# Two 64-row tiles for the logits and adjacency products of a two-step graph kernel

## The reference, cut to what matters

```
q = X @ W1.T @ W2.T;  k = X @ W3.T;  logits = q @ k.T          # width 64
probs = softmax(logits); keep the largest until their sum passes 0.9; A = renormalised
R = (adj + I) / rowsum(adj + I)
for n in (0, 1):
    A  = top_p_attention(Xa)
    Xf = R @ Xf;   Xa = A @ Xa
    Z += Xf @ U1[n].T + Xa @ U2[n].T
out = layernorm(x + layernorm(x + Z) * g + b)
```

## Time and profile before

| | |
|---|---|
| median of 3 runs | 1667.79 us (1663.79 to 1667.81) |
| profiled execution, its own time | 1664.64 us |
| its span, first to last instruction | 1662.8 us |
| TensorE busy | 1531.0 us, 92% |
| VectorE busy | 1266.9 us, 76% |
| ScalarE busy | 779.7 us, 47% |
| GpSimd busy | 244.0 us, 15% |
| mean granted TensorE clock | 0.956 of full |
| rank stage one, rank stage two | about 20 to 320 us, 786 to 1152 us |

### The profile page before, as it was taken

How to read it: one execution, slowest core, us unless ns; L and a number is a source line. 1 busy time by engine, 2 the same in 40 slices (tenths; PEclk the granted TensorE clock), 3 DMA queues, 4 the chain that set the end, 5 groups by cost and what they waited for, 6 DMA issues and landing times. The chain is left out here.

```text
span 1662.8 us, 17981 instructions
## 1 busy us (share of the span) xinstructions
PE 1531.0 (92%) x4753; PEld 887.4 (53%) x4753; DVE 1266.9 (76%) x3735; ACT 779.7 (47%) x1237; POOL 244.0 (15%) x283
## 2 busy tenths in 40 slices
PE   7999999979999999998999999998259879899996
PEld 4556556434555555554566666565135445455553
DVE  6788888723677777776799999999868787787664
ACT  4555555412556565564444444444134434445444
POOL 2010210241000000001001111112310221312222
PEclk9999999989999999998999999999569999999998
DMA  7556566644444555555556766672000000000000
GB/s 266 176 154 155 154 171 188 192 180 140 166 173 187 208 208 188 185 202 205 187 155 200 190 182 186 178 177 79 3 2 1 1 8 7 1 7 7 7 7 13
DMA packets 53452, 211.94 MB, mean 127 GB/s; under 512 B 22464, under 2 KB 31232, under 8 KB 32880
## 3 DMA queue, kind: packets, MB, share of 16 engines
q1 hardware_dynamic: 49872, 210.61, 40.7%
q0 software_dynamic: 3488, 0.31, 0.2%
HBM read 206.64 MB, written 4.50 MB: 127 GB/s over the span
## 5 line engine op out<-in xcount | busy, mean ns | idle before, releaser
L1289 ACT ACTIVATE psL<-psL,umax 128x1024 f32<-128x1024 f32 x256 | 278.5, 1088 | 297.1 <-DVE umax L1812 297.0
L1818 DVE MAX8 cand<-psL 128x8 f32<-128x256 f32 (+1 forms) x640 | 372.4, 584 | 57.4 <-PE psL L916 52.1
L915 PE MATMUL psL<-kA,mq 128*128 128x512 f32 x512 | 299.5, 585 | 2.5 <-ACT psL L1289 1.6
L885 PE MATMUL psO<-adj_in,xn 128*128 128x512 f32 x512 | 242.7, 597 | 3.8 <-DMA adj_in<-in_adjT 2.1
L885 PE MATMUL psO<-adj_in,xf 128*128 128x512 f32 x512 | 241.9, 597 | 4.4 <-POOL adj_in L611 4.4
L1097 PE MATMUL psO<-ebuf,xn 128*128 128x512 f32 x512 | 241.5, 593 | 0.5 <-DVE ebuf L2029 0.5
L2029 DVE SCALAR_TENSOR_TENSOR ebuf<-ebuf 128x1024 f32<-128x1024 f32 x128 | 156.7, 1225 | 109.0 <-PE psO L1097 92.2
L1449 ACT ACTIVATE ebuf<-psL 128x1024 f32<-128x1024 f32 x128 | 130.5, 1022 | 187.8 <-PE psL L1143 153.4
L916 PE MATMUL psL<-kB,mq 66*128 66x512 f32 x512 | 203.8, 398 | 0.0
L1398 ACT ACTIVATE ebuf<-psL 128x1024 f32<-128x1024 f32 x128 | 130.9, 1023 | 129.3 <-PE psL L1064 128.9
L1155 PE MATMUL psO<-xf,xa 128*128 128x512 f32 x340 | 167.6, 617 | 5.7 <-DVE xf L2182 5.6
(11 more groups left out here) (341 smaller groups left out, 1962.3 us busy)
## 6 DMA issues: line engine op xcount, KB each, us to landing
adj_in<-in_adjT SPq DMA_DIRECT2D x128, 1024.0 KB, 5.0
adj_in<-in_adj SPq DMA_DIRECT2D x32, 2048.0 KB, 7.6
xaT<-in_xT SPq DMA_DIRECT2D x4, 512.0 KB, 5.4
xa_dram<-xa SPq DMA_DIRECT2D x8, 256.0 KB, 7.8
out<-t SPq DMA_DIRECT2D x8, 256.0 KB, 2.3
list_dram<-ids,place POOLq DMA_INDIRECT x64, 9.3
rel_prob<-cut_dram SPq DMA_DIRECT2D x32, 2.0 KB
cut_dram<-ncut SPq DMA_DIRECT2D x16, 2.0 KB, 8.8
```

The costliest lines, as they stand in the source:

```text
L885: last = nc.tensor.matmul(psO[:], fs[:, j, :], adj_in[:, r % RING, j % JQ, :], start=(j == 0), stop=(j == JT - 1))
L915: nc.tensor.matmul(o, qA[:, t * P:(t + 1) * P], kA[:, c:c + BI], start=True, stop=False)
L1289: nc.scalar.activation(ps[:], ps[:], ACT.Exp, bias=umax[:, bass.ds(i * UB + k, 1)], scale=1.0, accum_out=usum[:, bass.ds(i * UB + k, 1)]). ...
L1818: last = v.max(cand[:, t % 2, at + c * 8:at + c * 8 + 8], psL[(turn + k) % 3][:, c * WIDE:(c + 1) * WIDE])
```

## The change

In both rank stages, logits and adjacency products are issued as matmuls of 64 rows on either half of the array, each half into a PSUM bank of its own.

- Logits: a unit is now six matmuls, three on partitions 0 to 63 into an even bank (the unit's first 512 columns) and three on partitions 64 to 127 into an odd bank (the second 512). `kB` grows to 128 partitions and holds, besides hi(k), the lo and hi parts in the half where each tile needs them; the lower half is put back with one copy (`k_restore`) at the stage's end, the rows of ones with a memset on GpSimd.
- Key units: a second ScalarE copy and a second VectorE difference for each; GpSimd's copy is half as wide.
- Adjacency: a call becomes two 64-row calls, into `psO` and `psO_odd`. ScalarE makes two copies at a group's end, and GpSimd adds them (`join_flow`, signal `r_o_sum`) before transposes or z terms read the flow. The two groups of step one outside the rank stage stay as they were.
- Banks: `psO_odd` takes a bank of the third unit buffer. Units take turns in two buffers, and TensorE waits for the exponential of unit k-2.
- Order: step one's transposes come three units later; the first block's adjacency counts in step two change to (0, 0, 2 x 5, 3 x 4, 2 x 5).

```diff
+        banks = pb("banks", [P, 6, BI])
+        psL = [banks[:, 2 * b:2 * b + 2, :].rearrange("p h c -> p (h c)") for b in range(3)]
         psO = pb("psO", [P, BI])
+        psO_odd = banks[:, 5, :]
+        def unit_banks(w):
+            first = 2 * ((w + 1) % 2)
+            return first, first + 1
...
+                def join_flow(i):
+                    pool.wait_ge(g["r_o_sb"], i + 1)
+                    pool.sem_inc(met, 1)
+                    flow = flowT[:, i * BI:(i + 1) * BI] if s == 0 else oT[:]
+                    nc.gpsimd.tensor_tensor(flow, flow, flow_odd, ALU.add).then_inc(g["r_o_sum"], 1)
...
+                JOIN_BEFORE = {0: 0, 1: 1, 3: 2, 4: 3, 5: 4, 7: 5}
...
-                    last = nc.tensor.matmul(psO[:], fs[:, j, :], adj_in[:, r % RING, j % JQ, :],
-                                            start=(j == 0), stop=(j == JT - 1))
+                    if s > 0 or i < FLOWS:
+                        low_rows = nc.tensor.matmul(psO[:], fs[0:DA, j, :], adj_in[0:DA, r % RING, j % JQ, :],
+                                                    start=(j == 0), stop=(j == JT - 1))
+                        high_rows = nc.tensor.matmul(psO_odd, fs[DA:P, j, :], adj_in[DA:P, r % RING, j % JQ, :],
+                                                     start=(j == 0), stop=(j == JT - 1))
...
+                def two_tiles(even, odd, hi, lo, u, landed):
+                    c = u * UNIT
+                    first, second = slice(c, c + BI), slice(c + BI, c + UNIT)
+                    low, high = slice(0, DA), slice(DA, P)
+                    nc.tensor.matmul(even, hi[low], kA[low, first], start=True, stop=False)
+                    nc.tensor.matmul(odd, hi[high], kA[high, second], start=True, stop=False)
+                    nc.tensor.matmul(even, hi[low], kB[low, second], start=False, stop=False)
+                    nc.tensor.matmul(odd, hi[high], kB[high, second], start=False, stop=False)
+                    nc.tensor.matmul(even, lo[low], kB[low, first], start=False, stop=True).then_inc(landed, 1)
+                    nc.tensor.matmul(odd, lo[high], kB[high, second], start=False, stop=True).then_inc(landed, 1)
...
-                            if not (prev is None and k < 3):
-                                pe.wait_ge(g["r_exp_done"], i * UB + k - 2)
+                            if i * UB + k >= 2:
+                                pe.wait_ge(g["r_exp_done"], i * UB + k - 1)
...
+                            even, odd = unit_banks(i * UB + k)
+                            two_tiles(banks[:, even, :], banks[:, odd, :], qA[:, t * P:(t + 1) * P], qB[:, t * P:(t + 1) * P],
+                                      u, g["r_l_ps"])
...
                 def k_hi(of, u):
                     act.wait_ge(of["k_ps"], u + 1)
-                    nc.scalar.copy(kA[:, u * UNIT:(u + 1) * UNIT], psL[k_bank(u)][:]).then_inc(of["k_act"], 1)
+                    nc.scalar.copy(kB[DA:P, u * UNIT + BI:(u + 1) * UNIT], banks[DA:P, k_banks(u)[1], :])
+                    nc.scalar.copy(halves_of(kA[:, u * UNIT:(u + 1) * UNIT]), bank_pair(k_banks(u))).then_inc(of["k_act"], 1)
+                def k_restore():
+                    nc.scalar.copy(kB_odd[0:DA, :, 1, :], kA_odd[0:DA, :, 1, :])
                 def rank_o_copy(i):
-                    act.wait_ge(g["adj_used"], i * PARTS + PARTS)
+                    act.wait_ge(g["adj_used"], 2 * (i * PARTS + PARTS))
+                    if s > 0 or i < FLOWS:
+                        if i > 0:
+                            act.wait_ge(g["r_o_sum"], i)
+                        nc.scalar.copy(flow_odd, psO_odd)
                     nc.scalar.copy(flowT[:, i * BI:(i + 1) * BI] if s == 0 else oT[:], psO[:]).then_inc(g["r_o_sb"], 1)
```

More of the change, by code:

```diff
@@ L275, in gnn_kernel, with bank_pair @@
         rest = ebuf[:, 0:N // UNIT, :].rearrange("p a b -> p (a b)")
-        psL = [pb(f"psL{b}", [P, UNIT]) for b in range(3)]
+        banks = pb("banks", [P, 6, BI])
+        psL = [banks[:, 2 * b:2 * b + 2, :].rearrange("p h c -> p (h c)") for b in range(3)]
         psO = pb("psO", [P, BI])
+        psO_odd = banks[:, 5, :]
+        def unit_banks(w):
+            first = 2 * ((w + 1) % 2)
+            return first, first + 1
+        def bank_pair(pair):
+            even, odd = pair
+            return banks[:, even:odd + 1, :]
         psT = pb("psT", [P, TB, D])
@@ L371, in flow_rows @@
             end = flow_window(a)[1]
-            fitting = [unit for unit in range(end + 1, NB * UB) if 4 <= unit % UB <= 8]
+            fitting = [unit for unit in range(end + 4, NB * UB) if 4 <= unit % UB <= 8]
             return fitting[0] if fitting else None
@@ L812, in _ @@
             pe.wait_ge(loaded_first, 16 * LOADS_FIRST)
-            nc.tensor.matmul(psQ[:, 0:DA], w1_sb[:], w2T_sb[:], start=True, stop=True).then_inc(w_ps, 1)
-            pe.wait_ge(w_sb, 1)
+            nc.tensor.matmul(psQ[:, 0:DA], w1_sb[:], w2T_sb[:], start=True, stop=True).then_inc(w_made, 1)
+            pe.wait_ge(w_made, 2)
             pe.wait_ge(ready, 2)
@@ L824, in k_unit @@
                     for hb in range(2):
-                        last = nc.tensor.matmul(psL[k_bank(u)][:, hb * BI:(hb + 1) * BI], wk[:],
+                        last = nc.tensor.matmul(banks[:, k_banks(u)[hb], :], wk[:],
                                                 xaT[:, (2 * u + hb) * BI:(2 * u + hb + 1) * BI], start=True, stop=True)
@@ L884, in adj_part @@
                             pe.wait_ge(g["self_in"], (i + 1) * TB)
-                    last = nc.tensor.matmul(psO[:], fs[:, j, :], adj_in[:, r % RING, j % JQ, :],
-                                            start=(j == 0), stop=(j == JT - 1))
-                    if j % JQ == JQ - 1:
-                        last.then_inc(g["adj_used"], 1)
-                def rank_block(i, prev, more, turn):
+                    if s > 0 or i < FLOWS:
[3 more added lines that the diff above has]
+                                                     start=(j == 0), stop=(j == JT - 1))
+                        if j % JQ == JQ - 1:
+                            low_rows.then_inc(g["adj_used"], 1)
+                            high_rows.then_inc(g["adj_used"], 1)
+                    else:
+                        last = nc.tensor.matmul(psO[:], fs[:, j, :], adj_in[:, r % RING, j % JQ, :],
+                                                start=(j == 0), stop=(j == JT - 1))
+                        if j % JQ == JQ - 1:
+                            last.then_inc(g["adj_used"], 2)
@@ L891, in adj_with, with rank_block @@
+                def rank_block(i, prev, more):
                     def adj_with(k):
-                        counts = (0,) + (2,) * 8 + (3, 3) + (2,) * 5
+                        counts = (0,) + (2,) * 8 + (3, 3) + (2,) * 5 if prev is not None else (0, 0) + (2,) * 5 + (3,) * 4 + (2,) * 5
                         assert len(counts) == UB and sum(counts) == JT
@@ L968, in tile_logits @@
                         pe.wait_ge(g["h_qlo"], r * PT + c + 1)
+                    if c == 0:
+                        if n == 2:
+                            pe.wait_ge(g["r_o_sb"], NB)
+                        return two_tiles(psL[bank][:, 0:BI], psL[bank][:, BI:UNIT], hqA, hqB, n, g["slot_full"])
                     for hb in range(2):
```

129 lines of the change are left out of this document (76 added, 53 removed).

## The result

The changed kernel takes 1698.63 us (median of 4 runs, 1698.12 to 1699.96) against 1667.8 us before (4 runs beside it, 1663.79 to 1668.06): ratio 1.0192, 95% interval 1.0177 to 1.0208. It is slower by 31 us; 10 were forecast. The profiled execution has a span of 1697.3 us against 1662.8, 34.5 us more.

| us | before | after | difference |
|---|---|---|---|
| start to first maximum | 20.7 | 24.8 | +4.1 |
| stage one | 296.6 | 304.8 | +8.3 |
| between the stages | 469.5 | 469.0 | -0.5 |
| stage two | 366.1 | 387.7 | +21.7 |
| behind it | 509.9 | 511.0 | +1.0 |

A forecast was written before the change was run, and what follows sets the result against it. TensorE was taken to bound stage one, TensorE and VectorE almost equally stage two. From 1664.64 us, -6.6 (stage one), +16 (stage two) and +3.5 (edges) sum to +12.9, say 1678 us; range 1642 to 1706.

The forecast's parts named there:

- The joins on GpSimd: Stage two: additions of some 2.2 us each, between copies and unit 3, cost nothing while GpSimd's queue is clear.
- Overlap: TensorE: array halves run together; a unit's logits take 0.70 us instead of 0.93, paired adjacency calls stay near 0.854.
- the lag: Adjacency calls: delay between weight load and matmul at each change of half; 0.7 us a block stage one, 0.5 stage two.
- Rival D: TensorE: the halves do not overlap; +28 and +35 us a block, near 2180 us; chance 0.04.
- C: TensorE: halves overlap but weight loads do not hide; +7.3 and +9.3 us a block, 1801 us; chance 0.10.
- Layout changes: TensorE, between half-array and full-array work: 0.08 us each, bounds 0 and 0.17; 0.5 us a block stage one, 0.7 stage two.
- Stage one: Eight blocks: logits saving -3.73, layout 0.5, two units in turn 1.7, lag 0.7; -0.83 a block, -6.6 us.
- Stage two: Eight blocks: walk +1.1, ScalarE copies +0.4, lag 0.5; +2.0 a block, +16 us.
- the walk: Stage two, unit by unit through a block: VectorE's 45.2 us plus 2.3 of waits, 47.5 against 46.4, +1.1.
- the two ScalarE copies: Stage two, block's end: two copies of 0.59 us ahead of exponential 15 delay next block's logits 1; +0.4 a block.
- Edges: Stage starts and restore copy: extra key-unit copies and differences expose some 1.2 us twice; 3.5 us, bounds 2 and 5.
- Rival B: Both stages: the saving is kept, VectorE's order shifts so two banks suffice; -32 us, 1632 us; chance 0.29.

The follow-up runs named there:

- mended kernel: Changed kernel with GpSimd's order altered: stage one's group-3 identity after join 2, stage two's first list fetched after join 6; 1686.82 us, ratio to before 1.0102.
- two-unit kernel: Kernel before with two logits units in turn instead of three, no tiles and no joins; 1698.59 us, ratio 1.0185.

## Why the prediction was right in direction and wrong in size

**The step that failed** is this one: "The joins on GpSimd (some 2.2 us each by its nearest row) lie between the copies and unit 3, more than 6 us, so they cost nothing while its queue is clear". The queue was not clear. Its order puts a wait for an adjacency slab and four list stores ahead of join 2 of stage one, and a wait for stored lists ahead of join 6 of stage two. I priced the addition (it takes 1.28, not 2.2) and not what stands in front of it, though I had named "joins queue behind GpSimd's list stores" as what would prove me wrong. Undone, it gives 14.7 + 4.9 = 19.6 us in the two blocks, though only 11.8 in the time, since the pauses and the stretch between the stages take the rest back. The profiles are 34.5 apart against a sum of 12.9, so the miss is 21.6, and this step is nine tenths of it. The rest is +0.2 in stage one, +0.8 in stage two, and 1.0 behind it.

**Overlap: right.** Logits of a unit in three slots and adjacency in 0.86 us a call; the lag (0.7 and 0.5 us a block) is not there. Rival D did not happen. Nor did C: the weight loads stay hidden. The Trainium skill, TensorE: Matmul & The Clock Gate, Part 3, had 3.07 times for four row tiles, a 77% efficiency; with two tiles this trace shows nothing lost, 0.43 us for a pair of passes.

**Layout changes: too cheap.** 0.08 was taken with an upper bound of 0.17; they cost 0.2, so 7.6 us for the 38 of stage one, where 4 were forecast. The trace agrees with the rule of the Trainium skill (TensorEngine Tiling (Array Packing), Key Properties) that a change of mode drains TensorE: each change shows 0.2 us that the same steps on the full array do not. The upper end that I had worked out for it was the better value.

**Stage one: the total is right, in part by luck.** Forecast -6.6 us, measured -6.4 with the joins mended. Measured apart, two units in turn cost 9.9 us and tiles give 16.3; 4.8 and 4.2 of these lie in the first block. In the other seven it is 0.72 a block for the former (1.7 forecast, with faster logits) and 1.73 for the latter (3.73 - 0.5 - 0.7 = 2.53 forecast). Both terms were too large by some 0.8 to 1.0, and the errors offset each other.

**Stage two: the total is right, the terms are not.** The first seven blocks are 14.2 us longer, 2.03 a block, against 2.0, made of 1.1 from the walk, 0.4 for the two ScalarE copies and 0.5 for the lag. Lag and copies cost nothing: units 15 and 0, around the copies, take what they took before. So the waits of VectorE cost about twice what the walk gave. Its places were right for the largest: it had waits of 0.3, 0.55, 0.2, 0.3 and 0.3 us ahead of units 4, 9, 10, 11 and 14, and 0.57, 1.02, 0.24, 0.32 and 0.18 are lost there (counted at the unit before each); at 13 and 15, with 0.15 and 0.1, nothing is lost. The two behind the z terms are twice as large as forecast. With 3.9 us of TensorE against 2.9 of VectorE at unit 8, and no stock, the prediction's own rule (what TensorE is late by is lost at once) gave 1.0, and not 0.55. What the walk did not try is to deal the calls out otherwise, which is worth 7.7 us in stage two.

**Edges: right only in sum.** 3.5 us were forecast; the start took 4.1 and not 1.2, since I missed that key unit 3 reuses the bank of key unit 1 and so waits for two copies and two differences. The stretch between the stages came out 0.5 shorter, helped by the clock (5.40 to 3.70 us for eight passes).

**Rival B** (the saving is kept) is refuted for stage two by the two-unit kernel alone. Its condition, bank returns under about 1 us a block in the mean of both stages, is missed there: 1.24 and 2.87, 2.05 in the mean.

Open: what makes VectorE pause at the turn of a block in the kernels with mended joins (the first seven blocks of stage two take 4 to 7 us longer than in the changed one, the calls being as they were), and why the clock falls behind stage one in some executions and not in others. The mended kernel's profiled execution, 1688.35 us, stays 10.8 above my sum: 5.4 in stage two, 3.8 at the edges, 0.2 in stage one and 1.5 behind the stages.

## What to carry to other kernels

An instruction added to a queue costs what stands ahead of it there: before pricing it at nothing, list the waits and stores in front of it and when each is met. A PSUM bank taken from a rotation costs a stock of finished work, and the price is paid at the units where the producer is the slower one; so deal its side work out evenly first, or make the change only in the stage where the consumer has slack (here stage one).

## What the runs showed of the hardware

- Two 64-row tiles run wholly side by side: a pair of fp32r matmuls every 0.23 us, a pair of float32 passes every 0.43 us, even where the two passes of the low half stand ahead of those of the high half in the code.
- Going from half-height tiles to the full array or back costs 0.2 us: about 0.1 at the step and 0.1 at the next one; 0.2 also as the mean over the 239 changes in stage one of the kernel with logits alone on tiles.
- After an 11 us stop of TensorE the passes started 0.85 us apart, the 1.2 GHz level (granted clock 0.50 from 192.85 to 198 us): the block took 13.6 us more than in the mended kernel, for a wait of 11.1. Behind a stop of 3 us the same program ran at this level in one execution and at 2.4 GHz in another.
